# xDeepFM on one core: first CIN layer in three fp32r terms instead of fp32, its low parts on GpSimd, deep weights split later

## What is computed

```
emb = tables[feat_idx, sparse]                      # 512 x 26 x 32
linear_out = lin_sparse_w[feat_idx, sparse].sum(-1) + dense @ lin_dense_w
xk = x0 = emb
for w, bb in ((conv1_w, conv1_b), (conv2_w, conv2_b)):
    hp = einsum('bhd,bmd->bhmd', xk, x0).reshape(-1, h * M, E)
    xn = sigmoid(einsum('oi,bid->bod', w, hp) + bb)
    xk, kept half = xn[:, :64], xn[:, 64:]
cin_out = (concat(kept halves).sum(-1) @ cin_w + cin_b)
h1 = tanh(concat(emb, dense) @ W1 + b1)             # 845 -> 1024
h2 = tanh(h1 @ W2 + b2)                             # -> 512
h3 = tanh(h2 @ W3 + b3)                             # -> 256
out = linear_out + cin_out + h3 @ deep_w + deep_b + bias
```

## Time and profile before

| | |
|---|---|
| time, median of 3 runs (lowest to highest) | 432.55 us (431.69 to 432.77) |
| the profiled execution's own time | 432.29 us |
| its span | 430.4 us |
| PE busy | 413.3 us, 96% |
| DVE busy | 320.0 us, 74% |
| POOL busy | 167.3 us, 39% |
| ACT busy | 161.0 us, 37% |
| mean granted clock of PE | 0.992 |
| period of a pair in the middle | about 20.0 us |

### The profile page before, as it was taken

One profiled execution on the slowest core, in us unless ns is written; L12 is line 12 of the kernel. 1 busy time (PEld: TensorE's weight loads), 2 busy tenths in 40 slices (PEclk: granted clock), 3 DMA queues, 4 the chain that ended last, 5 costly groups with the idle time before them and its releaser, 6 DMA issues. The chain is left out here.

```text
span 430.4 us, 5216 instructions
## 1 busy us (share of the span) xinstructions
PE 413.3 (96%) x1874; PEld 167.6 (39%) x1874; DVE 320.0 (74%) x356; ACT 161.0 (37%) x264; POOL 167.3 (39%) x146
## 2 busy tenths in 40 slices
PE   3978989999999999999999999999999999999997
PEld 1422323333333333333233333333333344886784
DVE  4115799898999799999798998998989895332121
ACT  3073252544544534535253544443543411111011
POOL 6663466664746584675540000000000193870000
PEclk9996999999999999999999999999999999999999
DMA  5357696888786898778887778675856720320000
GB/s 195 82 122 164 168 229 162 194 192 196 177 202 141 200 193 210 173 191 184 191 190 189 178 186 192 163 201 133 213 143 153 177 66 10 114 76 0 0 2 0
DMA packets 38304, 64.03 MB, mean 149 GB/s; under 512 B 19601, under 2 KB 22033, under 8 KB 38278
## 3 DMA queue, kind: packets, MB, share of 16 engines
q1 hardware_dynamic: 34694, 61.93, 58.3%
q0 software_dynamic: 3584, 1.76, 3.3%
HBM read 61.96 MB, written 1.71 MB: 148 GB/s over the span
## 5 line engine op out<-in xcount | busy, mean ns | idle before, releaser
L355 POOL DMA_INDIRECT emb<-in_table,rows x112 | 132.8, 1186 | 86.1 <-DMA emb<-in_table,rows 52.6
L730 DVE TENSOR_TENSOR prod<-ring,xk 128x1024 f32<-128x1024 f32 x112 | 132.7, 1217 | 29.2 <-PE ring L431 14.2
L730 DVE TENSOR_TENSOR copied<-copied,xk 128x1024 f32<-128x1024 f32 x96 | 115.4, 1242 | 0.5
L441 PE MATMUL conv<-prod,w_sb 128*64 128x512 f32 x448 | 112.2, 615 | 0.0
L441 PE MATMUL conv<-copied,w_sb 128*64 128x512 f32 x384 | 91.9, 594 | 1.5 <-DVE copied L730 1.5
L419 PE MATMUL conv<-sq,w_sb 117*64 117x512 f32 x384 | 88.1, 593 | 0.3 <-issue 0.3
L579 ACT ACTIVATE xk<-conv,const_sb 64x512 f32<-64x512 f32 x64 | 43.7, 683 | 97.2 <-PE conv L419 84.1
L376 POOL TENSOR_TENSOR xt_lo<-xt,xt_hi 128x512 fp32r<-128x512 f32 (+1 forms) x7 | 12.8, 1863 | 122.1 <-ACT xt_hi L640 122.1
L568 ACT ACTIVATE sq<-ring 117x512 f32<-117x512 f32 x90 | 48.6, 594 | 29.7 <-PE ring L403 23.5
L441 PEld LDWEIGHTS conv<-copied,w_sb 128*64 128x64 f32 x384 | 26.8, 137 | 57.6 <-issue 45.4
L419 PEld LDWEIGHTS conv<-sq,w_sb 117*64 117x64 f32 x384 | 27.2, 136 | 54.2 <-issue 53.4
(11 more groups left out here) (76 smaller groups left out, 299.2 us busy)
## 6 DMA issues: line engine op xcount, KB each, us to landing
copied<-laid SPq DMA_DIRECT2D x192, 256.0 KB
wpiece<-in_mlp SPq DMA_DIRECT2D x22, 256.0 KB
emb<-in_table,rows POOLq DMA_INDIRECT x112
raw<-laid SPq DMA_DIRECT2D x32, 52.0 KB
laid<-emb SPq DMA_DIRECT2D x16, 96.0 KB
sel_f<-in_sel SPq DMA_DIRECT2D x1, 832.0 KB, 5.7
const_sb<-in_const SPq DMA_DIRECT2D x1, 626.0 KB, 4.2
w_sb<-in_w SPq DMA_DIRECT2D x1, 416.0 KB, 6.3
```

What stands on the lines that cost most here:

```text
L355: pool.indirect_dma_start(out=emb[0:n, i, j, :], out_offset=None, in_=table, in_offset=bass.IndirectOffsetOnAxis(ap=rows[0:n, i, j:j + 1], ...
L441: mm = nc.tensor.matmul(conv[i % 2][c * HALF:(c + 1) * HALF, :], w2_sb[:, t, :], prod_of(r)[:, c, :], start=(t == 0), stop=(t == T2 - 1))
L730: nc.vector.tensor_tensor(prod_of(r)[:, :, :].rearrange("p c n -> p (c n)"), left[:, :, :].rearrange("p c n -> p (c n)"), xk[i % 2][:, :, ...
```

## The change

The change has these parts; each stands in the diff below, cut to its core.

1. Layer 1 in fp32r: ACT rounds each square to a high part `sq_hi` (`square_high`), GpSimd subtracts it from the square and leaves the low part in the square's place (`sq_low`; for pair 0 DVE does it), the weights are split once at the start, and `layer1` is nine matmuls with all 128 output columns: for each u high x high and low weights x high, and at the end the three with the low parts of the squares.
2. GpSimd's queue is written out: it waits until DVE has done 4, 8 and 12 products of a pair (the next two or three on DVE then read PSUM), does one, two and three low parts, and issues two, two and three of the seven gathers behind them. Where gathers end, other subtractions (deep weights, `xt_lo`) take their places.
3. PE's order: `sums_of` moves from in front of groups to places behind groups 0 and 1 and in front of group 2, the last two groups have 3 and 2 tiles, and `deep(0, 0)` stands behind group 2 of the last pair.
4. x's low part in one DVE operation for both halves; `raw` is now fetched four times for a pair (two more DMAs), a column of 0 and 1 in `small_sb` says which rows are low. SP fetches and lays out at other places.
5. Deep weights: 4 pieces of W1 are split in pairs 1 to 4 as before. The other ten are loaded in pairs 4 to 13 straight into their place, and split at the end: the first five by ACT and POOL in pairs 14 and 15, the second five by ACT and DVE behind the last pair.
6. The end: the aux row is one matmul at the start, read by ACT; the folded sums are weighted on DVE, and one matmul takes the place of the four; the last tile of the last layer, its tanh, the last matmuls and the last addition are done in halves of 256 columns.

```
-LAY_AT = 3
-DEEP_AT = 1
-GROUPS = ((0, 1, 2, 3), (4, 5, 6, 7), (8, 9, 10, 11), (12,))
+LAY_AT, FETCH_AT = 1, 4
+DEEP_AT = 2
+GROUPS = ((0, 1, 2, 3), (4, 5, 6, 7), (8, 9, 10), (11, 12))
-SUMS_IN = {0: ((1, 2),), 2: ((2, 0),), 3: ((2, 1),)}
+SUMS_BEFORE = {2: ((2, 2),)}
+SUMS_BEHIND = {0: ((2, 0),), 1: ((2, 1),)}
...
             def layer1(i, c):
...
                 for u in range(UT):
-                    pe.wait_ge(sq_done, squares_up_to(i, u, c))
-                    for q in range(2):
-                        o = slice(q * HALF, (q + 1) * HALF)
-                        mm = nc.tensor.matmul(l1_bank(i, c)[o, :], w1_sb[:, u, o], sq[i % 2][0:UK, u, c, :],
-                                              start=(u == 0), stop=(u == UT - 1))
+                    pe.wait_ge(sq_hi_done, squares_up_to(i, u, c))
+                    nc.tensor.matmul(bank[:, :], w1_hi[:, u, :], sq_hi[i % 2][0:UK, u, c, :],
+                                     start=(u == 0), stop=False)
+                    nc.tensor.matmul(bank[:, :], w1_lo[:, u, :], sq_hi[i % 2][0:UK, u, c, :],
+                                     start=False, stop=False)
+                for u in range(UT):
+                    if i:
+                        pe.wait_ge(sq_lo_done, lows_up_to(i, u, c))
+                    else:
+                        pe.wait_ge(sq_lo0_done, UT * c + u + 1)
+                    mm = nc.tensor.matmul(bank[:, :], w1_hi[:, u, :], sq_lo[i % 2][0:UK, u, c, :],
+                                          start=False, stop=(u == UT - 1))
...
         @block.gpsimd
...
+            def sq_low(i, u, c):
+
+                pool.wait_ge(sq_hi_done, squares_up_to(i, u, c))
+                nc.gpsimd.tensor_tensor(sq_lo[i % 2][0:UK, u, c, :], sq[i % 2][0:UK, u, c, :],
+                                        sq_hi[i % 2][0:UK, u, c, :].bitcast(F32), ALU.subtract)\
+                  .then_inc(sq_lo_done, 1)
...
+            for i in range(RX):
+                gather(i)
+            for u in range(UT):
+                for c in range(2):
+                    sq_low(1, u, c)
+                gather(RX, range(2 * u, 2 * u + 2 if u < UT - 1 else GJ))
             for i in range(NPAIR):
-                gather(i)
...
+                pool.wait_ge(prod_done, T2 * i + 4)
+                if 1 <= i and i + 1 < NPAIR:
+                    sq_low(i + 1, 2, 1)
...
+                pool.wait_ge(prod_done, T2 * i + 8)
+                if 1 <= i and i + 2 < NPAIR:
+                    sq_low(i + 2, 0, 0)
+                    sq_low(i + 2, 0, 1)
...
+                pool.wait_ge(prod_done, T2 * i + 12)
...
+                if i + 2 < NPAIR:
+                    sq_low(i + 2, 1, 0)
+                    sq_low(i + 2, 1, 1)
+                    sq_low(i + 2, 2, 0)
...
         @block.scalar
...
+            def square_high(i, u, c):
+
+                act.wait_ge(sq_done, squares_up_to(i, u, c))
+                nc.scalar.activation(sq_hi[i % 2][0:UK, u, c, :], sq[i % 2][0:UK, u, c, :], ACT.Copy)\
+                  .then_inc(sq_hi_done, 1)
...
         @block.vector
...
             def x_low(i):
 
                 dve.wait_ge(x_hi_done, i + 1)
-                for c in range(2):
-                    at = HALF * c
-                    nc.vector.tensor_tensor(x[i % RX][at + XLO:at + XK, :], raw[i % RX][at:at + M, :],
-                                            x[i % RX][at:at + M, :].bitcast(F32), ALU.subtract).then_inc(x_lo_done, 1)
+                nc.vector.scalar_tensor_tensor(x[i % RX][0:XEND, :], raw[i % RX][0:XEND, :],
+                                               small_sb[0:XEND, C_LOW:C_LOW + 1],
+                                               x[i % RX][0:XEND, :].bitcast(F32),
+                                               ALU.mult, ALU.subtract).then_inc(x_lo_done, 1)
...
+            for m in range(NL, 2 * NL):
+                src, _, _, lo = late(m)
+                dve.wait_ge(late_copied, m + 1)
+                dve.wait_ge(late_lo, m)
+                nc.vector.tensor_tensor(lo, src, lo.bitcast(F32), ALU.subtract).then_inc(late_lo, 1)
```

More of the change, by code:

```diff
@@ L38 @@
 GSEM = 4
+XEND = HALF + XK
 RING = 3
@@ L256, in build @@
                     enter(("spread", r))
+                for j, u in sums_of_group(SUMS_BEHIND, i, g):
+                    enter(("sums", j, u))
         def l1_bank(i, c):
@@ L465, in deep, with deep_halves @@
                 mm.then_inc(mlp_done, 1)
+            def deep_halves(layer, mt):
+                hi, lo, kt, xh, xl = deep_layers[layer]
+                n = sum(MT[:layer]) + mt
+                pe.wait_ge(tanh_done, n - 1)
+                for h in range(2):
+                    at = slice(h * BH, (h + 1) * BH)
+                    for k in range(kt):
+                        for j, (w, x_) in enumerate(((hi[:, k, :], xh), (lo(k), xh), (hi[:, k, :], xl))):
+                            mm = nc.tensor.matmul(half_bank[h], w[:, mt * P:(mt + 1) * P],
+                                                  x_[:, k, at], start=(k == 0 and j == 0),
+                                                  stop=(k == kt - 1 and j == 2))
+                    mm.then_inc(mlp_done, 1)
             pe.wait_ge(const_in, 16)
@@ L477, in _ @@
                                  start=True, stop=True)
+            pe.wait_ge(aux_in, 16)
+            nc.tensor.matmul(conv[1][0:1, :], small_sb[:, C_AUX:C_AUX + 1], aux[:, :], start=True, stop=True)\
+              .then_inc(aux_done, 1)
             pe.wait_ge(sel_done, 1)
@@ L569, in squares, with sigmoid @@
                       .then_inc(sq_done, 1)
-            def sigmoid(i, c):
+                for c in range(2):
+                    square_high(i, u, c)
+            def sigmoid(i, c, between=None):
                 bank = l1_bank(i, c)
```

317 lines of the change are left out of this document (228 added, 89 removed).

## The result

| | before | after |
|---|---|---|
| time, median | 432.12 us (431.45 to 432.77, 4 runs) | 459.17 us (458.59 to 460.3, 4 runs) |
| span of the profiled execution | 430.4 us | 458.5 us |
| period of a pair in the middle | 20.0 us | 20.9 to 23.6 us, three of 19.4 to 19.8 |

The ratio is 1.0642 (1.061 to 1.0673): the change makes the kernel 6% slower. The forecast of 422.4 us and its range up to 430.5 were wrong, and so was the sign.

A forecast was written before the change was run, and what follows sets the result against it. PE was taken to bound the kernel, with DVE 1.6 us per pair behind. The terms 3 - 12.3 + 1 + 0.5 - 1.9 - 0.3 = -10.0 us gave 422.4 us, range 415.5 to 430.5.

The forecast's parts named there:

- Layer 1 on PE: Nine fp32r matmuls instead of six fp32 ones gain 0.44 us per half: -12.3 us (-9.8 to -14.8).
- Rival C: Layer 1: going from sums to full matmuls and back costs 0.52 us instead of 0.09; 447 us, chance 0.04.
- Moving the sums: PE's order: sums and the tile going from group 2 to group 3 were said to cost nothing.
- What must keep up: Middle pairs: DVE and POOL should stay under PE's 19.1 us; +1 us in all for stalls (0 to +4).
- the lock: Middle pairs: a DVE operation with two SBUF inputs and a GpSimd subtraction block each other; 0.5 to 1.2 us per pair.
- meeting: Middle pairs: a low part on GpSimd falling on a copied product on DVE, costing DVE 1.2 us each.
- Rival B: Middle pairs: low parts falling on copied products make DVE the bound and the kernel slower, 442 us; chance 0.07.
- The start: Up to layer 1 (2, 0): begins at about 68.5 instead of 65.47, +3 us (+1 to +6).
- Two DMAs more per pair: Fetching: two more 52 KB DMAs per pair beside twelve of 256 KB were costed at nothing.
- The last pair: `deep(0, 0)` moves behind tile 10 and the wait for the last `xt_lo` goes: +0.5 us (-1 to +2).
- between the deep layers: 2.68 us of aux and fold matmuls become one matmul and a change of form: -1.9 us (-1.5 to -2.2).
- the end: Last tile as 24 matmuls of 256 columns, shorter matmuls, tanh and addition behind: -0.3 us (-1 to +1).

The follow-up runs named there:

- e1_gather2: Changed kernel with each pair's first gather waiting for the gathers of two pairs before instead of one; 446.82 us, ratio 1.0341.
- e2_no_low: Changed kernel without low parts of squares from pair 1 on, the third term of layer 1 reading high parts again; 434.59 us, ratio 1.0068.

## Why the prediction was wrong

The forecast was -10.0 us from the profiled execution, the span grew by 28.1. Of the 38.1 us between them 12.0 lie in the start, 8.4 in PE's own price of 13 pairs (19.78 instead of 19.1), 16.8 in DVE holding up PE there, and 0.9 in the rest. About 4 of the 16.8 us are the lower clock and not the waits themselves: in three of the pairs PE is busy 1.1, 1.2 and 1.9 us longer than at full clock (granted 0.94, 0.94, 0.90). Two slips in the sum change nothing here: the bounds add up to -18.0 and +1.7, so to 414 and 434 and not 415 and 433, and a pair before takes 20.01 us, not 20.02. By the steps of the prediction:

- **Layer 1 on PE: right.** I took 0.44 us per half, between 0.35 and 0.53. In equal order it is (20.70 - 19.78) / 2 = 0.46. Rival C's mechanism exists, but at 0.175 us for a change of form (next point) and not 0.52.
- **"Moving the sums ... doesn't change how many matmuls or group ends there are: nothing." Wrong**, and the first step that failed. The count was right, and it was the wrong count. What costs is a change of form between neighbours, 0.175 us each, or 0.18 to 0.19 by the steps inside the blocks: 8 in a pair before, 12 now, since sums stand alone in front of both halves of layer 1. Measured +0.70 us per pair with layer 1 in fp32, 9.1 us over 13 pairs; less 0.5 us that layer 1 gained beyond 0.44, that is the 8.4 to a rounding. I had one such change in the earlier trace rows at 0.09 and applied it to layer 1 alone. The Trainium skill, "TensorEngine Tiling (Array Packing)", section "Key Properties", says that changing the tiling mode drains TensorE; it gives no price. The runs here show a price at each such change, 0.69 us for four, which agrees with it; a drain as such no trace here shows.
- **What must keep up: the lock. I weighed it and priced it too low**, +1 us in all, measured 17.8 (13 pairs cost 14.8 more, though PE's own price of one is 0.23 less). The price of a meeting, 1.2 us, holds on average (beside three low parts in a row it was 3.4, the 4.65 us above). I checked that low parts fit beside products from PSUM if GpSimd begins on time, and wrote that "its waits put it back at each third of a pair". The waits only keep it from being early. What makes it late is its own first wait in `gather`, for the rows of the pair before, 41.2 us in all on the page. The earlier trace rows has it at 52.6 us, and my 10.3 us for seven gathers left it out. At 14 such waits in the trace before it is 3.8 us each, and GpSimd's queue is then 18.4 + 3.8 = 22.2 us, longer than the 19.1 us of the pair that it had to keep up with. That is where this step failed. When that wait is shortened, pairs fall to 19.78 us. In its places the work costs DVE 18.49 - 17.95 = 0.54 us per pair (e1_gather2 and e2_no_low, both pairs with a piece of deep weights; 17.90 and 17.34 without), at the low end of the 0.5 to 1.2 that I gave. Rival B, at 0.07, was the mechanism: copied products took (1.758 - 1.214) x 6 = 3.3 us more per pair in the middle, 2.7 meetings of 1.2 us, against a break-even of 2.5 (2.2, as DVE's own work is 17.34 us a pair, where I had 17.06). Its 442 us would have come out higher with the right start and the two blocks more.
- **The start: +3, measured +15.** I had GpSimd's low parts among its gathers, the fifth near 51 us (it was at 51.45), and wrote that "part is made up". It wasn't: DVE doing them saves 6.7 us. x's low part moved from behind product 5 to behind product 2 wasn't priced at all: in pair 1 DVE stands behind x's high part, which ACT does behind the squares, and PE waits 3.92 us; with it back at 5 the start is 70.3. Of the remaining 4.8 us, 4.1 are there at the first product (35.17 against 31.09), where I had said 2.3; with layer 1 in fp32, without high and low parts, it comes at 32.43, so 2.7 of them go with the parts of pair 0's squares. By the runs the 15.0 us split thus: 5.4 are there with layer 1 in fp32 (70.9), 3.0 more without low parts from pair 1 on (73.9), 6.6 more with them.
- **Two DMAs more per pair at nothing**: nothing in the changed kernel speaks against it, and ACT waits less for `raw` than before (4.7 us in all, 50.0 before). Where x is wanted earlier, in two of the experiments, the fetch is the last to come.
- **The last pair, between the deep layers, the end: right.** +0.6 for the last pair against -0.4 was the only small miss. The pieces between the layers are one of 0.52 us where there were 2.68, -2.2. The 24 matmuls of 256 columns take 2.87 us, at half the stream and not at the weight load:

```profile
426.32 0.52 PE ring L683 x2
...
451.77 2.87 PE ring L606 x24
```

The Trainium skill's rule that I cited ("SBUF — State Buffer", "Who interferes with whom") holds in all of this: a copied product, two inputs in SBUF, waits for a low part on GpSimd to end, one from PSUM stays at 1.22 us. It was weighed by whether the places fit, when the question was what keeps GpSimd in them.

Still open: what holds up ACT while many gathers are in flight at the start. That it goes away with the wait is shown (449.54 against 435.94; x's low part was moved in the same step, but pair 1's first sums, which lie ahead of it, begin at 51.2 and 37.9 in the two profiles). That ACT waits for its own instructions to be fetched is not borne out by that trace: among its DMA packets none of kind "instruction" lies between the start of the span and 58.61 us, when the hold-ups are over.

## What to carry to other kernels

Work moved to an engine whose operations hold up those of a busier one (here GpSimd and DVE) gains only as long as it is done in its place: list every wait in the queue that it joins and add it to that queue's length, since a wait that was free there becomes the bottleneck's. When an order is changed with "the same instructions", count the changes of form between neighbours, not the instructions. And a queue with 18.4 us of work in a period of 19.1 can't take a wait of 3 us, whatever its busy share says.
